# FFN1 of a fused attention and quantized FFN layer: w1's blocks fetched back ahead of the store of h, and turned as VectorE's first work of a tile

## The reference, cut to what matters

```python
def _ste_quant_rows(a):
    scale = max(max|a| over the row / 127, 1e-8)
    return clip(round(a / scale), -127, 127) * scale
def _linear8bit(x, W, b):
    outlier = (max |x| over all tokens, per column) > 3.0
    return quant_rows(where(outlier, 0, x)) @ quant_rows(W).T + where(outlier, x, 0) @ W.T + b
h = _linear8bit(xn, W1, b1)        # W1: 2048 x 512      "FFN1"
y = _linear8bit(h, W2, b2)         # W2: 512 x 2048      "FFN2"
out = x + attention(xn) * silu(y)
```

## Time and profile before

| what | value |
|---|---|
| median of 3 runs | 801.87 us |
| the profiled execution, its own time | 802.13 us |
| its span, from the first to the last instruction | 800.4 us |
| around the span | 1.73 us |
| TensorE busy | 756.8 us (95%) |
| VectorE busy | 650.9 us (81%) |
| ScalarE busy | 395.4 us (49%) |
| GpSimd busy | 274.5 us (34%) |
| mean granted clock of TensorE | 0.981 |

### The profile page before, as it was taken

The page is one execution under the profiler, slowest core; times in us unless marked ns, Lnnn a source line. Parts: engine busy times, 40 slices in busy tenths (PEclk is TensorE's granted clock), DMA queues, the critical chain, the costliest instruction groups (busy, mean ns, idle before and its releaser), DMA issues. The chain is left out here.

```text
span 800.4 us, 11979 instructions
## 1 busy us (share of the span) xinstructions
PE 756.8 (95%) x4133; PEld 569.1 (71%) x4133; DVE 650.9 (81%) x1115; ACT 395.4 (49%) x670; POOL 274.5 (34%) x349
## 2 busy tenths in 40 slices
PE   5999999999999999999998998899997999999995
PEld 4878665556776767766576876688886788888884
DVE  7988999999999899995536585686868998599957
ACT  4354167767676667777633354355453333132212
POOL 7213135555555555554622112122200000036504
PEclk9999599999999999999999999999999999999999
DMA  7421303323222223334455857646332778436982
GB/s 265 146 106 53 81 21 89 82 81 95 82 83 83 82 82 100 88 108 134 158 184 141 253 149 180 171 99 149 77 71 73 270 216 263 165 106 219 307 315 105
DMA packets 115276, 110.71 MB, mean 138 GB/s; under 512 B 71808, under 2 KB 71824, under 8 KB 113680
## 3 DMA queue, kind: packets, MB, share of 16 engines
q1 hardware_dynamic: 115216, 109.95, 46.5%
HBM read 56.43 MB, written 40.37 MB: 121 GB/s over the span
## 5 line engine op out<-in xcount | busy, mean ns | idle before, releaser
L933 DVE TENSOR_REDUCE rowmax<-ps 128x2 f32<-128x512 f32 (+3 forms) x384 | 210.4, 591 | 19.6 <-PE ps L1010 18.0
L854 ACT ACTIVATE probs<-ps 128x512 f32<-128x512 f32 (+1 forms) x352 | 174.8, 558 | 71.3 <-PE ps L1023 70.0
L1010 PE MATMUL ps<-km,stack 128*128 128x256 f32 (+3 forms) x512 | 149.7, 347 | 2.2 <-PEq L195 1.9
L1023 PE MATMUL ps<-stack,ks 128*128 128x512 f32 (+1 forms) x352 | 131.4, 383 | 2.8 <-ACT probs L854 2.7
L1010 PEld LDWEIGHTS ps<-km,stack 128*128 128x128 f32 (+1 forms) x512 | 94.2, 197 | 43.2 <-DVE rowmax L933 23.8
L836 POOL TENSOR_SCALAR_AFFINE_SELECT probs<-probs 128x512 f32<-128x512 f32 x128 | 81.0, 641 | 78.3 <-ACT probs L854 77.1
L1861 PE MATMUL ps<-big_h 128*128 128x512 f32 x256 | 99.9, 390 | 2.0 <-issue 1.6
L1863 PE MATMUL ps<-big_h,big_l 128*128 128x512 f32 x256 | 99.6, 389 | 0.0
L1862 PE MATMUL ps<-big_l,big_h 128*128 128x512 f32 x256 | 99.6, 389 | 0.0
L1036 PE MATMUL ps<-probs,vones 128*32 128x512 f32 (+3 forms) x1024 | 82.2, 439 | 0.2 <-POOL probs L836 0.2
L1023 PEld LDWEIGHTS ps<-stack,ks 128*128 128x128 f32 x352 | 66.5, 189 | 11.7 <-ACT probs L854 6.2
(11 more groups left out here) (227 smaller groups left out, 1375.5 us busy)
## 6 DMA issues: line engine op xcount, KB each, us to landing
stack<-big_h SPq DMA_DIRECT2D x128, 64.0 KB, 2.0
h_scratch<-hs SPq DMA_DIRECT2D x7, 1024.0 KB, 4.5
hload<-h_scratch SPq DMA_DIRECT2D x14, 512.0 KB, 5.1
xn_scratch<-xa SPq DMA_DIRECT2D x4, 1024.0 KB, 4.4
stack<-big_l SPq DMA_DIRECT2D x64, 64.0 KB, 2.0
xi<-xn_scratch SPq DMA_DIRECT2D x16, 256.0 KB, 2.7
xe_scratch<-xm SPq DMA_DIRECT2D x16, 256.0 KB, 2.3
w2n<-in_L_ffn_W_dram SPq DMA_DIRECT2D x4, 1024.0 KB, 6.0
```

The costliest lines, as they stand in the source:

```text
L854: nc.scalar.activation(probs[p][:, o:o + nh * w], ps[:, STB[n % NST], 0:nh * w], ACT.Exp).then_inc(s_exp, 1)
L933: nc.vector.tensor_reduce(dst, src, AX_X, ALU.max).then_inc(s_red, 1)
L1010: last = nc.tensor.matmul(dst, stack[u % 3][rows, hp, P * qt:P * (qt + 1)], km[rows, u // KT, p0:p0 + npar, keys], start=True, stop=True)
L1023: ins = nc.tensor.matmul(ps[:, STB[n % NST], 0:nh * w].rearrange("p (h q) -> p h q", h=nh), ks[:, u // KT, p, P * kt:P * (kt + 1)], stack[ ...
```

## The change: what it does

On SyncE the four DMAs that fetch the blocks back move from the head of an iteration to a place ahead of the store of h, and there they fetch the blocks of tile f+2 rather than f+1. So the blocks of a tile are fetched one iteration earlier in the list, right behind the store of the same tile's rounded rows and behind the stores of W2's pieces.

On VectorE `turn_w1(f + 1)` moves from behind `scale_w1(f + 2)` to the head of iteration f, ahead of `feature_max(f - 1)` and `scale_w1(f + 2)`. In iteration 0 `scale_w1(2)` moves ahead of `low_w1(1)`. No instruction is added or removed.

```diff
@@ SyncE, the loop over tiles
                 for f in range(FT):
-                    if 2 <= f + 1 < FT:
-                        load_w1_blocks(f + 1)
                     if f + 3 < FT:
                         load_w1(f + 3)
...
                     for q in w2_pieces(f):
                         store_w2(q)
+                    if f + 2 < FT:
+                        load_w1_blocks(f + 2)
                     if f < SPILL:
                         sp.wait_ge(s_he, NC * (f + 1))
                         sp.dma_start(h_d[f, :, :], hs[f % 2][:, :]).then_inc(s_hst[f % 2], 16)
@@ VectorE, the loop over tiles
                     if f == 0:
                         for i in range(EARLY, NT):
                             low_x(i)
+                        scale_w1(2)
                         low_w1(1)
+                    if 2 <= f + 1 < FT:
+                        turn_w1(f + 1)
                     if f:
                         feature_max(f - 1)
-                    if f + 2 < FT:
+                    if f and f + 2 < FT:
                         scale_w1(f + 2)
-                    if 2 <= f + 1 < FT:
-                        turn_w1(f + 1)
                     if f % KT == 0:
                         scale_w2(f // KT)
```

## The result

The changed kernel takes 845.44 us (median of 4 runs, 844.97 to 846.14), the kernel before 801.69 on the same chip (4 runs). The ratio is 1.0546, with a 95% interval of 1.0517 to 1.0574: slower, by 43.8 us. The profiled execution took 846.14, against 846.3 predicted.

What follows compares the result with a forecast made beforehand. The prediction took TensorE's matmuls as the bound, with 14.4 us of FFN1 lost to waits and what follows them. The new loop moved FFN1's end from 603.9 to 648.1, +44.2 us on 802.13: 846.3, range 836 to 860.

Steps and rivals of the forecast that it cites:

- closes a loop: FFN1: turn, maxima, scaling, rounding, store, fetch, next turn wait on each other; 15.5 us a tile against TensorE's 11.2.
- The least that the rows allowed: FFN1, shortest turn-to-turn distance: 6.3 + 2.0 + 4.35 = 12.7 us, for three iterations of thirteen.
- The loop's length: FFN1, time from one tile's turn to the next: 13.5 to 17.0 us by W2 work, 201.7 us over thirteen iterations.
- GpSimd's low part: FFN1: it waits for the next tile's rounding, then takes 1.3 us; a tile starts 7.7 us behind its turn.
- The slow matmuls: FFN1, TensorE: after a wait eight or so matmuls 0.43 us apart cost 1.6 us, counted only in tile 14.
- The third rival: FFN1: TensorE's clock stays at 1.2 GHz, 20.5 us a tile, 923 us in all; chance 4%.
- My picture of some 3 us before each tile: FFN1: TensorE waits some 3 us before nearly every tile from 2 to 14, released by GpSimd's low part.
- The sum: FFN1's last matmul ends at 648.1 rather than 603.9: +44.2 us on the profiled 802.13, or 846.3.
- the start: FFN1: early scaling of tile 2 lets its turn begin at 430.1, 3.9 us earlier than before, gained once.
- The other rivals: FFN1 without waits, 787.7 us, 2%; no change that can be told, 2%; the loop at its upper bounds, beyond 860, 6%.
- its upper bounds: FFN1, fourth rival: slower blocks and landings in the same loop, 846 + 20 = 866 us; beyond 860, chance 6%.
- the first rival: FFN1: earlier blocks remove the waits and TensorE bounds it, 802.1 - 14.4 = 787.7 us; chance 2%.

Runs made afterwards that it cites:

- opening it at the turn: Changed kernel with VectorE's turn of tile f+1 put back behind the scaling of tile f+2: 787.83 us, ratio 0.9834 to the kernel before.
- VectorE's half alone: Kernel before with only the change's VectorE diff (turn first, early scaling of tile 2), SyncE's list as before: 863.08 us, ratio 1.0763.
- two edits that each shorten it: Two runs against the changed kernel: feature maxima moved behind the scaling, 828.88 us; blocks fetched ahead of the stores of W2's pieces, 822.58 us.
- together with GpSimd's: Changed kernel with maxima behind the scaling, blocks ahead of W2's stores and GpSimd's low part ahead of the rounding: 808.76 us, ratio 1.0083.
- GpSimd's list alone: Changed kernel with GpSimd's low part of tile f+1 ahead of the rounding of tile f+2: 843.71 us, ratio 1.0521 to the kernel before.
- SyncE's half alone: Kernel before with only the change's SyncE diff, blocks of tile f+2 ahead of the store of h: 791.22 us, ratio 0.9875.

## Why the prediction was right

**That the change closes a loop, and where.** Shown by the runs: opening it at the turn gives 787.8; VectorE's half alone closes it (863); two edits that each shorten it give back 17 and 23 us, and together with GpSimd's they give 37. GpSimd's list alone, though its low part ended every wait, is worth about 2 us. The least that the rows allowed was 12.7 us from turn to turn, and the shortest measured is 12.64.

**The loop's length.** By class, predicted and measured (the mean over the changed kernel's turns):

| iteration | predicted | measured |
|---|---|---|
| two pieces of W2 | 15.4 | 15.6 |
| one piece and w2n's load | 16.2 | 16.1 |
| none | 13.5 | 13.1 |
| the scaling of W2 | 17.0 | 16.7 |
| sum of thirteen | 201.7 | 200.0 (428.69 to 628.66) |

The store of the rounded rows came 6.27 us behind the turn (428.69 to 434.96); I had 6.3. The blocks took less where h no longer stood in front: 4.4 from issue to turn behind eight stores (439.90 to 444.28).

**GpSimd's low part: a term mis-sized.** I took 1.3 us from the earlier trace rows. In GpSimd's timeline of the changed kernel it takes 3.3 in ten of fourteen tiles and 1.3 in four:

```profile
450.54 3.31 POOL L1420 TENSOR_TENSOR w_low_second<-w1t_second,w_high_second 128x512 fp32r<-128x512 f32 x1
...
479.73 1.30 POOL L1420 TENSOR_TENSOR w_low_second<-w1t_second,w_high_second 128x512 fp32r<-128x512 f32 x1
```

So a tile starts 9.6 us behind its turn (613.15 to 622.72), not 7.7. As the loop sets the time, those 2 us count once, at tile 14.

**The slow matmuls: right in kind, low in size.** A wait of 6.00 was followed by eleven starts some 0.43 apart, not eight, and tile 14 took 13.5 us and not 12.8. The third rival did not come: the clock returned within each tile. The waits of 1.93 to 2.19 before tiles 3, 7 and 11 left no slow matmul. The length of the wait does not settle it: in the runs above, a wait of 1.87 (SyncE's half alone) was followed by seven matmuls 0.42 to 0.43 apart, and one of 3.01 (the maxima behind the scaling) by none. My picture of some 3 us before each tile was wrong in its pattern: seven waits of 4.4 to 6.0 before the even tiles, three of 2 before odd ones, none before tiles 5, 9 and 13, which come behind the short iterations, nor before tile 15, as forecast.

**The sum.** From FFN1's first matmul to its last I had 240.0 and it is 240.0 (407.46 to 647.50). That it agrees to 0.1 is luck, for the terms do not: the turn of tile 14 came 2.6 us early (0.8 at the start, the rest in the loop), the low part added 1.9 and the slow matmuls 0.7. The other rivals fell as they stood: no wait-free FFN1, and the loop not near its upper bounds.

**The order of load and wait.** The sentence of the Trainium skill ("DMA: Bandwidth & Descriptors", "Rules for kernel authors") that I set beside the change is borne out on both sides: the early issue with the late wait gives 0.9834 (787.83 us, the time of the first rival), the same issue with the early wait 1.0546. By the first reading above, early means here no more than ahead of one store of h.

## What to carry to other kernels

A wait put at the head of an in-order engine's list makes everything behind it depend on that wait: before moving one, follow the list on and ask whether anything behind it feeds the very transfer that it waits for. If it does, add the loop up and compare it with the bound engine's time a tile; over it the difference is paid in every tile (here 15.4 against 11.2 in the mean). That the move is free where the loop is shorter is what this would mean, but no run here shows it: the shortest loop built still took 12.7. And the engine that ends the bound engine's wait need not be the one to mend: the chain in order of time shows the loop, and here, moving the messenger was worth about 2 us of 44.

## What the runs showed of the hardware that I had not expected

GpSimd's low part, a subtraction of 128x512, takes 3.3 us beside one of VectorE's instructions and 1.3 beside others. In all ten slow cases VectorE was running the maximum of two tensors (L1608, the running maximum) when it started, and in all ten it ended 1.1 us behind that maximum. In the four quick cases VectorE ran a reduction (three) or a 32x32 transpose of W2. VectorE pays as well: the running maximum takes 2.98 to 3.19 us in six tiles, where GpSimd's rounding had already begun, and never more than 2.29 in the kernel before. In VectorE's timeline of the changed kernel, beside GpSimd's 450.54 above:

```profile
449.72 3.00 DVE L1608 TENSOR_TENSOR absmax<-absmax,habs 128x2048 f32<-128x2048 f32 x1
```

With the low part first, the low part no longer meets the running maximum and takes 1.27 us in the median; the rounding still meets it, and the running maximum takes up to 3.21. The Trainium skill, "GPSIMD Engine Reference", in its table of specifications, has the two engines share their access to SBUF, with contention when VectorE's instruction has two SBUF inputs; the running maximum has two, and the trace agrees.

From first issue to use, four transfers of 64 KB took 4.4 us with no megabyte just ahead of them in the queue, 5.8 behind a store of 1 MB (428.19 to 433.95), 7.1 behind a load of 1 MB (453.72 to 460.85) and 10.7 behind one of each (459.02 to 469.76).
